# Row sums of two attention branches added up on the Pool engine, with two units in one product run and single buffers for the exact pass's operands

## The reference

```python
def _attn(q, k, v, mask=None):
    s = jnp.einsum('bhqd,bhkd->bhqk', q, k) / np.float32(np.sqrt(HD))
    if mask is not None:
        s = jnp.where(mask, s, jnp.float32(-1000000000.0))
    return jnp.einsum('bhqk,bhkd->bhqd', jax.nn.softmax(s, -1), v)
...
o1 = _attn(q, k1, v1, causal[None, None])          # all 1024 keys, causal
...
o2 = _attn(q, ks, vs)                              # 256 selected keys
...
winmask = causal & (ii[:, None] - ii[None, :] < WINDOW)
o3 = _attn(q, kw, vw, winmask[None, None])         # the last 64 keys
g = gate[:, :, None, None, None]
o = g[:, 0] * o1 + g[:, 1] * o2 + g[:, 2] * o3
o = o.transpose(0, 2, 1, 3).reshape(B, T, N_HEAD * VDIM)
return o @ Wproj
```

## Time and profile before

| | |
|---|---|
| median of 3 runs | 2779.24 us (2778.72 to 2779.59) |
| the profiled execution | 2781.34 us, span 2779.4 us |
| PE busy | 2320.6 us, 83% of the span |
| DVE busy | 1628.3 us, 59% |
| ACT busy | 1266.2 us, 46% |
| POOL busy | 669.8 us, 24% |
| granted clock of TensorE, mean | 0.908 of full speed |

### The profile page before, as it was taken

One profiled execution on the slowest core, in us unless ns is written; L12 is line 12 of the kernel. 1 busy time (PEld: TensorE's weight loads), 2 busy tenths in 40 slices (PEclk: granted clock), 3 DMA queues, 4 the chain that ended last, 5 costly groups with the idle time before them and its releaser, 6 DMA issues. The chain is left out here.

```text
span 2779.4 us, 45396 instructions
## 1 busy us (share of the span) xinstructions
PE 2320.6 (83%) x16656; PEld 1545.5 (56%) x16656; DVE 1628.3 (59%) x3043; ACT 1266.2 (46%) x2777; POOL 669.8 (24%) x687
## 2 busy tenths in 40 slices
PE   5585858663999999999999999999999999601995
PEld 3464545442666666666666666566566666401884
DVE  4758575734466466466566576566565564450766
ACT  2354545440455555555455455555555555310442
POOL 0265656573011011011011011011010010145332
PEclk9697978765999999999999999999999999655997
DMA  2255555479547646556655565664664660611113
GB/s 97 97 219 184 216 187 201 172 269 226 126 93 146 132 101 139 122 118 131 127 121 122 120 136 114 136 129 104 137 137 96 138 130 10 158 39 47 48 53 110
DMA packets 222841, 360.53 MB, mean 130 GB/s; under 512 B 68794, under 2 KB 124701, under 8 KB 222240
## 3 DMA queue, kind: packets, MB, share of 16 engines
q1 hardware_dynamic: 216288, 348.43, 50.1%
q0 software_dynamic: 4320, 8.43, 0.9%
q10 hardware_dynamic: 2016, 0.77, 0.2%
HBM read 229.58 MB, written 126.56 MB: 128 GB/s over the span
## 5 line engine op out<-in xcount | busy, mean ns | idle before, releaser
L1370 ACT ACTIVATE prob<-ps 128x512 f32<-128x512 f32 (+5 forms) x1600 | 637.8, 441 | 665.8 <-PE ps L1325 656.3
L1434 DVE TENSOR_REDUCE maxima<-ps 128x1 f32<-128x512 f32 (+3 forms) x768 | 387.5, 547 | 291.4 <-PE ps L1250 147.0
L1344 PE MATMUL ps<-prob,plain 128*32 128x512 f32 (+5 forms) x3200 | 512.0, 443 | 0.0
L1400 POOL TENSOR_TENSOR products<-products,sums 128x256 f32<-128x256 f32 x192 | 140.8, 733 | 1540.3 <-DVE sums L1425 1539.0
L1439 DVE TENSOR_REDUCE maxima<-ps 128x2 f32<-128x512 f32 (+1 forms) x512 | 293.7, 606 | 192.6 <-PE ps L1261 98.4
L1425 DVE RECIPROCAL sums<-sums 128x256 f32<-128x256 f32 x192 | 331.9, 1736 | 97.6 <-ACT sums L1383 97.6
L1317 PE MATMUL ps<-q1a_s,k1a_s 128*128 128x512 f32 (+3 forms) x768 | 303.0, 395 | 0.0
L1325 PE MATMUL ps<-q1b_s,k1b_s 128*128 128x512 f32 (+3 forms) x768 | 301.1, 393 | 0.0
L1344 PE MATMUL ps<-prob,v_s 128*32 128x512 f32 (+3 forms) x1536 | 284.3, 491 | 0.0
L1250 PE MATMUL ps<-k1a_s,q1a_s 128*128 128x512 f32 (+3 forms) x768 | 234.5, 374 | 0.5 <-DVE maxima L1439 0.2
L1381 ACT ACTIVATE products<-ps,gates_a 64x512 f32<-64x512 f32 x192 | 131.0, 682 | 196.4 <-PE ps L1344 196.3
(11 more groups left out here) (333 smaller groups left out, 4889.8 us busy)
## 6 DMA issues: line engine op xcount, KB each, us to landing
qh_dram<-pairs SPq DMA_DIRECT2D x96, 512.0 KB, 2.7
kwh_dram<-pairs SPq DMA_DIRECT2D x64, 512.0 KB, 2.7
qa_s<-qh_dram SPq DMA_DIRECT2D x128, 256.0 KB, 4.7
kwa_s<-kwh_dram SPq DMA_DIRECT2D x128, 256.0 KB, 7.7
q1a_s<-qh_dram SPq DMA_DIRECT2D x128, 256.0 KB, 4.8
qb_s<-qh_dram SPq DMA_DIRECT2D x64, 256.0 KB, 9.3
kwb_s<-kwh_dram SPq DMA_DIRECT2D x64, 256.0 KB, 10.3
k1a_s<-k1ah_dram SPq DMA_DIRECT2D x32, 512.0 KB, 6.9
```

The lines of the kernel that those rows point to most:

```text
L1344: mm = pe.matmul(ps[at:at + VD, SCORES + k % 2, q0 - c * CH:q0 - c * CH + w], w_, m.prob[:, n % PROBS, h, 0:w], start=first, stop=True, sk ...
L1370: act.activation(m.prob[:, u % PROBS, h, 0:w], ps[:, turn % SCORES, 0:w], ACT.Exp, scale=SCALE).then_inc(s["exp_done"], 1)
L1400: pool.tensor_tensor(o, o, m.sums[:, br, cc], ALU.mult).then_inc(s["divided"], 1)
L1434: ins = dve.tensor_reduce(partial[:, h, i, part:part + 1], bank[:, 0:w], AX, ALU.max)
```

## The change

Five things are edited.

- *Order of units.* The window branch comes first (9 units). Behind it the units of branch 1 (both halves) and of branch 0's first half are paired one by one with those of branch 0's second half, of the same width each. `SUMS`, `LAST` and `LOCAL` follow.
- *Products.* For branches 0 and 1 the matmuls with `plain` are gone from each unit. The value matmuls of the two units of a pair run together in the four column groups (`products(side, group)`), the first unit in partitions 0 to 63 of its bank, the second in 64 to 127 of its own. The window branch is as before.
- *Row sums.* POOL adds the exponentials of a branch and half up in `acc` (steps `acc`, 12 a side). When all are in, PE multiplies `acc` with `plain` once (`total`, a fill in a spare bank) and ACT copies the sums out (`take`). Divisions of branch 1 follow in the same side; `total` of branch 0, its divisions and projections go to the next side (`closing`). ACT may overwrite a place of `prob` only when POOL has read it; the ring has 6 places instead of 4.
- *Buffers.* `qb`, `kwb`, `ksb`, `vw` and `vs` have one buffer instead of two.
- *Loads.* `window_exact` and `window_keys` wait for the window units of the side before, `local_exact`, the rows and then `local` for all units up to the end of branch 1.

The diff, cut to its core:

```diff
+SUMS = [(2, 0), (2, 1), (1, 0), (1, 1), (0, 0), (0, 1)]
...
+def groups():
+    found = units()
+    sets = [found[2, c][i:i + 2] for c in range(NC) for i in range(0, len(found[2, c]), 2)]
+    short = found[1, 0] + found[1, 1] + found[0, 0]
+    return sets + [list(x) for x in zip(short, found[0, 1])]
...
-SUMS = [(1, 0), (2, 0), (1, 1), (2, 1), (0, 0), (0, 1)]
-UNITS = units()
+UNITS = sum(groups(), [])
+TOGETHER = [tuple(UNITS.index(x) for x in group) for group in groups()]
 LAST = [max(u for u, x in enumerate(UNITS) if x[:2] == k) for k in SUMS]
-LOCAL = LAST[3] + 1
+LOCAL, WINDOWED = LAST[3] + 1, LAST[1] + 1
...
-PROBS = 4
+PROBS = 6
...
-    if w % 2 == 0 and w > 0:
-        pieces = [("divide", w - 1, len(SUMS) - 1, piece) for piece in range(PIECES)] + [("proj", w - 1, 1)]
+    if w > 0:
+        pieces = closing(w - 1)
     for u in range(len(UNITS) + 1):
         if u < len(UNITS):
             todo.append(("scores", w, u))
...
+            todo += [("acc", w, op) for op, x in enumerate(SUMMING) if x[0] == u]
+        ready = [group for group, follower in zip(TOGETHER, TOGETHER[1:] + [(len(UNITS),)]) if follower[0] == u]
+        for group in ready:
+            todo.append(("products", w, group))
+            for done in sorted(LAST.index(x) for x in group if x in LAST):
+                todo.append(("sum", w, done))
+                if SUMS[done][0] == 2 and w % 2 == 1:
+                    pieces += [("divide", w, done, piece) for piece in range(PIECES)]
+                if SUMS[done] == (1, NC - 1):
+                    pieces += total_and_divide(w, 1)
         todo += pieces[:1]
         pieces = pieces[1:]
-    return todo + pieces
+    return todo + pieces + (closing(w) if w == SIDES - 1 else [])
...
+def total_and_divide(w, br):
+    pieces = [("total", w, br), ("take", w, br)]
+    for c in range(NC):
+        if w % 2 == 1:
+            pieces += [("divide", w, SUMS.index((br, c)), piece) for piece in range(PIECES)]
+            if br == 0:
+                pieces.append(("proj", w, c))
+    return pieces
...
+def closing(w):
+    return total_and_divide(w, 0)
...
+    m.acc = sb("acc", [P, 2, NC, HP, CH])
...
             for side in range(1, SIDES):
+                units_done(side - 2, len(UNITS))
                 whole(side)
+                units_done(side - 1, WINDOWED)
+                window_exact(side)
+                if side + 1 < SIDES:
+                    window_keys(side + 1)
+                units_done(side - 1, LOCAL)
+                local_exact(side)
+                for br in (2, 1):
+                    row(side, br)
                 if side + 1 < SIDES:
                     local(side + 1)
-                for br in (2, 1, 0):
-                    row(side, br)
+                row(side, 0)
...
+                elif kind == "total":
+                    pe.wait_ge(s["acc_done"], len(SUMMING) * side + max(n for n, x in enumerate(SUMMING) if x[1] == a[0]) + 1)
+                    for c in range(NC):
+                        for h in range(HP):
+                            at = c * NW + h * VD
+                            mm = pe.matmul(bank[at:at + VD, :], m.plain[:], m.acc[:, a[0], c, h, :], start=True, stop=True,
+                                           skip_group_check=True)
...
+            def product(side, u, at, weights):
...
+                for h in range(HP):
+                    mm = pe.matmul(ps[at + h * VD:at + (h + 1) * VD, bank_of(side, k), q0 - c * CH:q0 - c * CH + w],
+                                   weights[h], m.prob[:, n % PROBS, h, 0:w], start=first, stop=True,
+                                   skip_group_check=True)
+                return mm
...
+                    if br == 2:
+                        product(side, u, 0, values)
+                        mm = product(side, u, NW, [m.plain[:]] * HP)
+                    else:
+                        mm = product(side, u, NW * place, values)
+                    mm.then_inc(s["products_done"], 1)
...
+                        old_side, old = divmod(u - PROBS, len(UNITS))
+                        if old in RELEASED:
+                            act.wait_ge(s["acc_done"], len(SUMMING) * old_side + RELEASED[old])
...
+                if kind == "take":
...
+                    for c in range(NC):
+                        ins = act.copy(m.sums[rows, br, c * CH:(c + 1) * CH],
+                                       ps[c * NW:(c + 1) * NW, 8 - SPARES + n % SPARES, :])
+                    ins.then_inc(s["taken"], 1)
...
+            for step in plan.of(("divide", "acc")):
+                if step[0] == "acc":
...
+                    pool.wait_ge(s["exp_done"], HP * (n + u + 1))
...
+                    if former is None:
+                        pool.wait_ge(s["acc_done"], len(SUMMING) * side + op)
+                        ins = pool.tensor_tensor(total, total, new[:, :, 0:w], ALU.add)
+                    else:
...
+                        ins = pool.tensor_tensor(total, old[:, :, 0:w], new[:, :, 0:w], ALU.add)
+                    ins.then_inc(s["acc_done"], 1)
```

More of the change, by code:

```diff
@@ L2 @@
 from contextlib import ExitStack
+from itertools import accumulate
 import numpy as np
@@ new lines, in window_exact @@
+            def window_exact(side):
+                src, g, own = kept[side // NSIDE], side % NSIDE // 2, side % NSIDE
+                for at, comp in ((0, 1), (32, 3)):
+                    sp.dma_start(m.kwb[at:at + 32].bitcast(F32), two(src.kw[g, comp], side)).then_inc(s["exact"], 16)
+                sp.dma_start(m.vw[:], src.vw[:, :, NW * own:NW * (own + 1)].rearrange("t p n -> p t n"))\
+                    .then_inc(s["exact"], 16)
+            def local(side):
+                k, src, g = side % 2, kept[side // NSIDE], side % NSIDE // 2
@@ L1161, in local @@
-                    sp.dma_start(m.ksb[at:at + 32, k].bitcast(F32), two(src.ks[g, comp], side)).then_inc(keys, 16)
-                vv = slice(NW * own, NW * (own + 1))
-                sp.dma_start(m.vw[:, k], src.vw[:, :, vv].rearrange("t p n -> p t n")).then_inc(s["late%d" % k], 16)
-                sp.dma_start(m.vs[:, k], src.vs[:, :, vv].rearrange("t p n -> p t n")).then_inc(s["late%d" % k], 16)
+                    sp.dma_start(m.ksb[at:at + 32].bitcast(F32), two(src.ks[g, comp], side)).then_inc(s["exact"], 16)
@@ L1309, in scores @@
                     elif br == 1:
-                        kx, ky = m.ksa[:, k, h, jj], m.ksb[:, k, h, jj]
+                        kx, ky = m.ksa[:, k, h, jj], m.ksb[:, h, jj]
                     else:
-                        kx, ky = m.kwa[:, k, h, jj], m.kwb[:, k, h, jj]
+                        kx, ky = m.kwa[:, k, h, jj], m.kwb[:, h, jj]
                     turn = HP * n + h
@@ new lines, in product, with products @@
+                return mm
+            def products(side, group):
+                pe.wait_ge(s["exp_done"], HP * (side * len(UNITS) + group[-1] + 1))
+                for place, u in enumerate(group):
+                    br, c, j = UNITS[u][:3]
+                    if br == 0:
+                        once("late%d" % (side % 2), 16 * LATE * turn_no(side))
+                        values = [m.v1[:, side % 2, j, :]] * HP
+                    else:
+                        once("exact", 16 * EXACT * (side + 1))
+                        values = [(m.vs if br == 1 else m.vw)[:, j, h * VD:(h + 1) * VD] for h in range(HP)]
+                    if br == 2:
+                        product(side, u, 0, values)
+                        mm = product(side, u, NW, [m.plain[:]] * HP)
+                    else:
+                        mm = product(side, u, NW * place, values)
+                    mm.then_inc(s["products_done"], 1)
```

187 lines of the change are left out of this document (110 added, 77 removed).

## The result

| | before | after |
|---|---|---|
| median | 2779.41 us (2778.72 to 2784.69) | 2891.75 us (2887.08 to 2898.53), 4 runs |
| ratio, 95% interval | | 1.0402 [1.0377, 1.0426] |
| profiled execution, span | 2781.34 us, 2779.4 us | 2891.55 us, 2889.7 us |
| mean granted clock | 0.908 | 0.875 |

The direction was forecast, the size was not: 2836 was said, 56 us less than came, and 2891.75 lies 12 us above the upper end of 2880.

A forecast was written before the change was run, and what follows sets the result against it. The prediction took PE's own work to bound the attention stage. From the profiled 2781.3 us, -112 (PE), +129 (waits), +45 (clock), -6 (start) and +1 (end) gave 2838; it said 2836 us, range 2725 to 2880.

The forecast's parts named there:

- the slow clock: After the two waits where an odd side turns even, and possibly at the projections: 3 us a pair, +45 us.
- PE's saving: Products and sums on PE, units of branches 0 and 1 two to a run: 3.6 us a side, -112 us.
- the end of the stage: Last side, bound by POOL's adds and divisions: 55 us to the last add to t2 against 54.3, +1 us.
- the start: Start of the attention stage: a smaller burst of loads ahead of the first rows, -6 us.
- The waits: Odd side's end and middle, even side's start: 10.9 us a pair against 2.3, +129 us over 15 pairs.
- The second fall: Clock falling again at the projections: an even chance, worth some 3.4 us of work.
- Loads: Split loads into single buffers stay hidden, with 3 us to spare; without that cover each microsecond late costs 31 us.
- POOL is hidden: Rival, 8 in 100: POOL has room for all its work, only PE's time counts: 2662 us.
- Only the odd side's waits come: Rival, 15 in 100: no waits before the projections and the clock holds; 6.4 us of waits a pair, 2724 us.
- All waits come, the clock stays: Rival, 17 in 100: all the forecast waits without a slow clock, 2791 us.
- POOL and DVE slow each other: Rival, 6 in 100: POOL's chains at both sides' ends a tenth longer, +35 us, 2871 us.
- The single buffers come late: Rival, 6 in 100: loads 3 us beyond the spare ones in each of 31 sides, 2929 us.

The follow-up runs named there:

- ballast: The changed kernel with idle matmuls put ahead of PE's waits at `rows`, `total` and the projections; 2826.53 us, 1.0164.
- late_ballast: proj_late with idle matmuls ahead of `rows` and `total` alone; 2779.48 us, 0.9994.
- proj_late: The changed kernel with an odd side's two projections moved from the 5th and 8th window unit of the next side to the 10th and 11th; 2816.45 us, 1.0117.
- no_adds: The changed kernel without POOL's adds of exponentials, `acc` set once to a constant (row sums wrong); 2844.51 us, 1.0227.
- div_moved: proj_late with branch 1's four divisions moved behind the first four window units of the next side; 2834.76 us, 1.0188.
- loads_early: loads_alone with the second group of loads waiting for 15 instead of 20 units of the side before; 2778.06 us, 0.9984.
- loads_alone: The kernel before with only the change's single buffers and split loads, the second group waiting for 20 of 25 units; 2806.41 us, 1.0092.
- mid_divisions: spare_products with the last side's adds on DVE and the divisions of branch 2's second half five units later; 2735.58 us, 0.9834.
- spare_products: div_moved with a second place for branch 2's products; 2748.44 us, 0.9879.
- late_no_adds: proj_late without POOL's adds, `acc` set once (row sums wrong); 2772.76 us, 0.9965.

## Why the size was wrong

**The sum.** The mechanism held: every wait came at the place and from the chain that was named, and the clock fell among them. What failed are the sizes of three terms: +45 us for the slow clock came at about +67, -112 us for PE's saving at about -92, and +1 us for the end of the stage at +13. For the steady pairs the prediction has -112 + 129 + 45 = +62 us; they took +105.6. The end has +13.2 for +1, the start -8.5 for -6. By pair, with `ballast` as the changed kernel at full clock (108.07):

| us a pair | forecast | measured |
|---|---|---|
| PE's own work | 96.0 | 97.3 |
| waits | 10.9 | 10.8 |
| slow clock | 3.0 | 4.5 |
| sum | 109.9 | 112.6 |

The 97.3 are an estimate: a stretch of one side without a projection takes 47.37 us (1498.33 to 1545.70, from one side's first unit of branch 1 to the next side's), about 0.5 of it waits for exponentials, and two projections add some 1.7 us each. The waits are the rest of 108.07. Over 15 pairs the clock is 22 us beyond its term, PE's own work 20, and the end 12.

**The clock.** The step that failed here is "a stretch of slow clock of about 7 us behind them" of which "1.3 us is left". The stretch was 10.2 us, and of it 2.9 us were left, the time from `total` to the first projection of 11.0 us against 8.1 in `ballast`. The second fall was taken as an even chance of losing 3.4 us, so 1.7 us. It came in every pair and cost 1.6 us: a right number out of a chance too low and a price too high, which is luck. `ballast` measures the two at 4.5 us a pair (68 us over 15; the medians differ by 65); `late_ballast` the first alone, in `proj_late`, at 2.4, 37 us. The prediction also saw the fall as the work of two waits close together; it follows the first of them, DVE's. Its guess of the length came from a row that shows only that a fall outlasts 1.7 us. The term's own upper end of 70 us held, but that alone takes 2838 to 2863, and with the end's 12 us and PE's 20 it comes out above the 2880 at which the range stopped.

**PE's own work** was put at 96.0 us a pair and is about 97.3, for 103.3 before: some 20 us over the stage. The product runs came as forecast (1.00, 0.78, 0.57 and 0.36 us for 0.98, 0.75, 0.54 and 0.33; `total` 0.97), so it isn't these. Unit 24's step takes 1.18 us for 0.73; 0.37 of it is a wait for ACT's exponentials, which half the product work no longer covers. Where the rest lies isn't shown.

**The end** was put at +1 and came at +13.2. The chain was seen (POOL's adds, `total`, `take`, four reciprocals, projections) but timed from rows at full clock, where `total` and the projections now run at half (1.93 us for 0.97), and with the last add too early: POOL ends at 2480.97. 11 us of it are owed to the adds, as `no_adds` shows (tail 447.1 for 458.1), and the divisions and projections behind them run in series.

**The waits were right**, for the changed kernel at either clock. At the odd side's end 5.0 was said. From the fills behind unit 18 to `total` PE takes 17.29 us, 12.51 in an even side: 4.8, with 2.10 at `rows` where 2.2 was said. The slow clock ahead of `total` adds nothing, since POOL's last add sets its start; `ballast` has 4.7 for the same stretch from branch 1's `total` on. POOL's chain took 16.3 us for 16.2. At the projections 1.8 and 2.6 were said, 1.43 and 2.31 came; in the middle of the odd side 1.6 for 1.4. That is 10.1 us; the rest of the 10.8 is PE's waiting for exponentials, which the forecast didn't list among the waits, so 10.8 for 10.9 looks closer than it is. `proj_late` takes the projections' waits away and shortens the even side, `div_moved` those of the turn, and its odd side falls from 52.2 to 49.1 us. Three slips in the prediction changed little: its four waits add up to 10.8, 0.63 is 0.23 us longer than 0.40, and 22 and 6 us are 53% of a side, not 60%; POOL was busy for 51% of the time from 1000 to 1200 us.

**Loads.** That the single buffers are hidden held (`loads_early`), with the price of a lost lead shown by `loads_alone`. The start gave 8.5 us for 6, but that doesn't confirm its term: the first exponential came only 2.05 us earlier (697.63 for 699.68), and in the profiles of the experiments it lies anywhere from 691.5 to 700.3.

**The rivals.** *POOL is hidden* fell: with room for all of it on average, its order still made the wait. *Only the odd side's waits come* fell by the 3.7 us at the projections. *All waits come, the clock stays* was the nearest miss; `ballast` is that case, 2827 for the 2791 said, the difference being PE's 20 us and the end's 12 in the main. *POOL and DVE slow each other* fell: reciprocals have a median of 1743 ns (1742 before) beside POOL's adds, the multiplies a mean of 728, and the 1024-wide add 2.37 us for 2.34. *The single buffers come late* fell.

**Where the gain went.** PE did get rid of 6 us of work a pair. The change puts the new sums and the divisions into narrow places of strictly ordered queues, so that 8.5 us of waits were added (10.8 for 2.3), and 4.5 us of slow clock behind them: 7.0 us a pair more. With the same work in other places (`mid_divisions`) the pair takes 102.4 and the kernel is 1.7% faster than before.

What stays open: where PE's own 1.3 us a pair lie, and which of the waits of `spare_products` at the start of even sides could still go.

## What to carry

Work moved to an engine that is idle on average isn't free: find the last instruction that a strict queue waits for, and lay out the chain ahead of it, step by step, at the two or three places where the consumer asks. When a wait of about 2 us goes into a stage that PE filled at full clock, price the wait and then the slow stretch behind it as a term of the same order (here 4.5 us for 8.5 of added waits); idle matmuls in the waits measure it in one run. And when a step is moved, look up which buffer it still holds at its new place: `div_moved` lost in that way what `spare_products` won with one more buffer.

## What the hardware showed

- The clock fell at the end of a wait of 2.10 us and stayed at 1.2 GHz for 10.2 us although PE was busy for 8.78 of these. A second wait of 1.21 us lies within this stretch; without it (`late_no_adds`) the clock falls too, for 3.4 or 6.8 us. In `proj_late` the two waits hold the stage at 0.96; matmuls of no use in them bring it back to 1.00, 37 us.
- The length of a wait alone doesn't tell whether the clock falls. In `after` it fell behind the 2.31 us ahead of the second projection, not behind the 1.43 ahead of the first. In `loads_alone` it stayed at 1.00 behind a wait of 2.44 us (ended at 967.98) and fell for 3.4 us behind one of 1.83 (ended at 2146.81).
- The Trainium skill's "TensorE: Matmul & The Clock Gate", section "Why this matters for your kernels", has a rule that PE should have no idle gaps beyond a certain length. None of the waits of the changed kernel's steady stage, 2.31 us at most, is that long, and the clock fell twice a pair; here the measurement decides.
- POOL's two-input adds ran beside DVE's reciprocals and reductions at their own pace, 2.37, 1.83, 1.28 and 0.73 us for 1024, 768, 512 and 256 elements a partition: by these rows about 2.1 ns an element and 0.2 us to begin. Its copy of 256 took 0.40 us, for the 0.32 taken.
